# One decoder stack kernel: the late part of the last layer's shared expert, its sums, its loads and its last stores rearranged

## The reference, cut to what matters

```python
logits = x @ router_w.T                      # 8 experts, 2 chosen for each token
combine = ...                                # weight of each expert for each token, 0 if not chosen
out_e = silu(x @ gate_w[e]) * (x @ up_w[e]) @ down_w[e]          # 352 hidden columns
moe_out = sum over e of combine[:, e] * out_e
shared = silu(x @ s_gate_w + s_gate_b) * (x @ s_up_w + s_up_b) @ s_down_w + s_down_b   # 704 hidden columns
x = x + tanh(g_ffn[1]) * (moe_out + shared)  # x on the right inside is layernorm(x)
```

## Time and profile before

| | us |
|---|---|
| median of 3 runs | 1297.12 (1293.11 to 1299.21) |
| the profiled execution | 1299.26 |
| its span | 1297.6 |
| late part: first gate matmul to the end of the span | 1224.70 to 1297.6 |
| granted TensorE clock, mean over the span | 0.94 |

### The profile page before, as it was taken

How to read it: one execution, slowest core, us unless ns; L and a number is a source line. 1 busy time by engine, 2 the same in 40 slices (tenths; PEclk the granted TensorE clock), 3 DMA queues, 4 the chain that set the end, 5 groups by cost and what they waited for, 6 DMA issues and landing times. The chain is left out here.

```text
span 1297.6 us, 19278 instructions
## 1 busy us (share of the span) xinstructions
PE 1101.2 (85%) x6093; PEld 524.5 (40%) x6111; DVE 758.0 (58%) x1420; ACT 665.2 (51%) x1010; POOL 459.9 (35%) x503
## 2 busy tenths in 40 slices
PE   0567688897689999999999658699979999999894
PEld 0334444453324234334323124354446655556441
DVE  6888876764786675575565356644434454452245
ACT  6888887795235665565575625231314434434320
POOL 1101433322300422323323410616328888870071
PEclk9987899998779999999999878889989999999998
DMA  9125800000102112011010022104644444442484
GB/s 322 67 97 146 316 1 2 1 1 9 59 24 58 40 31 75 27 30 45 25 35 21 18 76 67 45 2 155 258 135 156 146 147 148 150 145 81 142 287 153
DMA packets 70653, 121.37 MB, mean 94 GB/s; under 512 B 16996, under 2 KB 30692, under 8 KB 70072
## 3 DMA queue, kind: packets, MB, share of 16 engines
q1 hardware_dynamic: 61032, 88.38, 20.9%
q0 software_dynamic: 9264, 31.92, 7.5%
q10 hardware_dynamic: 288, 0.20, 0.1%
HBM read 73.81 MB, written 38.65 MB: 87 GB/s over the span
## 5 line engine op out<-in xcount | busy, mean ns | idle before, releaser
L1240 ACT ACTIVATE prob<-p_col,mask_col,any_key 128x512 f32<-128x512 f32 x256 | 185.8, 778 | 110.4 <-PE p_col L1371 108.9
L1438 DVE CUSTOM_DVE_ANT_0 ajunk<-p_row,mask_row 128x512 bf16<-128x512 f32 x256 | 166.9, 685 | 72.3 <-PE p_row L1321 71.9
L1334 PE MATMUL p_out<-prob,v 128*64 128x512 f32 x512 | 139.0, 621 | 0.1
L1321 PE MATMUL p_row<-ks,early_place 99*128 99x512 f16 x256 | 100.4, 395 | 13.3 <-DVE top L1438 12.1
L1160 POOL TENSOR_TENSOR o<-sum_a,rec 32x512 f32<-32x512 f32 x30 | 37.9, 1264 | 195.1 <-DMA rec<-inv_d 193.0
L1371 PE MATMUL p_col<-early_place,ks 101*128 101x512 f16 x256 | 96.1, 388 | 0.8 <-ACT prob L1240 0.3
L2373 DVE SCALAR_TENSOR_TENSOR shid<-s_up,ssilu 128x352 f32<-128x352 f32 x39 | 20.5, 525 | 118.3 <-PE s_up L2286 118.3
L2308 PE MATMUL s_down<-mw,shT 128*128 (+1 forms) x351 | 82.2, 379 | 1.1 <-ACT shT L2231 1.1
L2286 PE MATMUL s_gate<-mw,sxT 128*128 x468 | 78.3, 318 | 4.2 <-ACT sxT L2237 3.3
L2375 DVE TENSOR_TENSOR shidr<-shid,shidr 128x352 f16<-128x352 f32 x39 | 66.9, 1715 | 21.5 <-ACT shidr L2221 21.5
L2286 PE MATMUL s_up<-mw,sxT 128*128 x468 | 77.4, 316 | 0.0
(11 more groups left out here) (318 smaller groups left out, 2220.3 us busy)
## 6 DMA issues: line engine op xcount, KB each, us to landing
x_slots<-nought SPq DMA_DIRECT2D x3, 3328.0 KB, 20.8
xin<-x_slots SPq DMA_DIRECT2D x39, 256.0 KB, 2.7
y_slots<-y SPq DMA_DIRECT2D x39, 256.0 KB, 2.1
early_place<-in_ctx SPq DMA_DIRECT2D x8, 1024.0 KB, 5.7
mstg<-in_L_ffn_gate_w POOLq DMA_DIRECT2D x7, 704.0 KB, 4.9
mstg<-in_L_ffn_up_w POOLq DMA_DIRECT2D x7, 704.0 KB, 5.1
x<-in_x SPq DMA_DIRECT2D x4, 1024.0 KB, 7.4
w<-in_L_ffn_w SPq DMA_DIRECT2D x1, 4096.0 KB, 18.4
```

The source lines that it names most:

```text
L1240: nc.scalar.activation(prob[s % 4][:, c, :], p_col[c][:], ACT.Exp, bias=mask_col[:, b, k:k + 1], scale=any_key[:, b:b + 1]).then_inc(t_exp, 1)
L1321: nc.tensor.matmul(p_row[g % 2][:], qs[0:ROWS_R, j, g, t * P:(t + 1) * P], ks[b % 2][0:ROWS_R, g, :], start=True, stop=True).then_inc(t_ro ...
L1334: mm = nc.tensor.matmul(p_out[pr][c * 2 * DH:(c + 1) * 2 * DH, :], v1[b % 2][:, k, g, :], prob[n % 4][:, c, :], start=(k == 0), stop=(k == ...
L1438: nc.vector.tensor_tensor_reduce(junk[:, g % 2, :], p_row[g % 2][:], mask_row[:, blk // HPG, :], 1.0, -3e38, ALU.add, ALU.max, top[blk % 2 ...
```

## The change

- SP: `first_up`, a new buffer, gets the first 128 up columns of unit 0 at the stage's start in two DMAs of 128 KB, whose rows in memory are 256 bytes long. The wait for the last down product is gone. The store of the last `y` is issued ahead of the up weights of unit 0. The last batch's result goes out in two stores of 512 KB.
- PE: the first up group reads `first_up`. Down sums both units of a token tile in one bank: 18 matmuls for tile 0, then tile 1, 2 and 3. The four sums have a bank each, the two of `p_down` and the two of `p_gate`. Ahead of the first of them PE waits for all six hidden groups and for both units' down weights.
- DVE: four adds in place of eight, two behind `combine(1)` and two behind `combine(2)`. The last `combine` is done in two halves of two token tiles.

```diff
+    first_up = sb(st, "first_up", [P, 2, KB, P], F16)
...
+    late_sum = [*p_down, *p_gate]
...
             sp.dma_start(first_gate[:], shared_d[0, :, :, G0:U0]).then_inc(e_pre, 16)
+            for h in range(2):
+                sp.dma_start(first_up[:, h, :, :], shared_d[0, :, h, U0:D0].rearrange("p (k i) -> p k i", i=EI)[:, :, 0:P]).then_inc(e_pre, 16)
...
             body(PAIRS_OF_TILES, 0)
-            sp.wait_ge(e_down, TILES)
+            store(PAIRS_OF_TILES, 0)
             sp.dma_start(late_w[0][:, :, U0:D0], shared_d[0, :, :, U0:D0]).then_inc(e_lu, 16)
-            store(PAIRS_OF_TILES, 0)
             sp.dma_start(late_w[1][:, :, G0:D0], shared_d[1, :, :, G0:D0]).then_inc(e_lv, 16)
...
-            for b in range(B):
+            for b in range(LATE_B):
                 sp.wait_ge(e_sum, b + 1)
                 sp.dma_start(out_d[b], x[:, b * TPB:(b + 1) * TPB, :]).then_inc(e_out, 16)
-            sp.wait_ge(e_out, 16 * B)
+            for half in range(2):
+                t0 = half * TPB // 2
+                sp.wait_ge(e_sum, LATE_B + half + 1)
+                sp.dma_start(out_d[LATE_B][:, t0:t0 + TPB // 2, :],
+                             x[:, LATE_B * TPB + t0:LATE_B * TPB + t0 + TPB // 2, :]).then_inc(e_out, 16)
+            sp.wait_ge(e_out, 16 * (B + 1))
...
+                        here = n == 0 and (at == G0 or m == 0)
+                        if here:
+                            pe.wait_ge(e_pre, 16 * 5)
+                        else:
+                            pe.wait_ge(*((e_lu, 16) if n == 0 else (e_lv, 16)))
...
-            late_down(0, e_ld0)
-            late_down(1, e_ld1)
+            pe.wait_ge(e_ld0, 32)
+            pe.wait_ge(e_ld1, 32)
+            pe.wait_ge(e_hl, TILES + 2 * EB)
+            pe.wait_ge(e_y, TILES)
+            for t in range(TPB):
+                for n in range(2):
                     for m in range(EB):
                         for hs, hm in passes:
-                            mm = nc.tensor.matmul(p_down[t % 2][:], late_hT[n][hs][0:rows(m), m, t * P:(t + 1) * P],
+                            mm = nc.tensor.matmul(late_sum[t][:], late_hT[n][hs][0:rows(m), m, t * P:(t + 1) * P],
...
+                                                  start=(n + m + hs + hm == 0), stop=(n == 1 and m == EB - 1 and hs == 1))
+                mm.then_inc(e_down, 1)
...
+            def combine(b, t0=0, t1=TPB):
...
             combine(1)
             late_add(0)
+            late_add(1)
             combine(2)
-            late_add(1)
-            dve.wait_ge(e_y, TILES + 2 * TPB)
-            combine(LATE_B)
+            late_add(2)
+            late_add(3)
+            dve.wait_ge(e_y, TILES + TPB)
+            combine(LATE_B, 0, TPB // 2)
+            combine(LATE_B, TPB // 2, TPB)
```

More of the change, by code:

```diff
@@ L2334, in late_gate_up @@
                     c = EB * n + m
[L2335 to L2338, removed]
+                    for at, bank, done, free in ((G0, p_gate, e_gate, e_silu), (U0, p_up, e_up, e_hid)):
+                        here = n == 0 and (at == G0 or m == 0)
[3 more added lines that the diff above has]
+                            pe.wait_ge(*((e_lu, 16) if n == 0 else (e_lv, 16)))
                         pe.wait_ge(free, TILES + max(c - 1, 0))
-                        src = first_gate if n == 0 and at == G0 else late_w[n]
                         for k in range(KB):
@@ L2343, in late_gate_up @@
                                 q = at + k * EI + m * P
-                                mm = nc.tensor.matmul(bank[c % 2][0:rows(m), :], src[:, hs, q:q + rows(m)], late_T[hm][:, k, :],
+                                if n == 0 and at == G0:
+                                    lhs = first_gate[:, hs, q:q + rows(m)]
+                                elif here:
+                                    lhs = first_up[:, hs, k, :]
+                                else:
+                                    lhs = late_w[n][:, hs, q:q + rows(m)]
+                                mm = nc.tensor.matmul(bank[c % 2][0:rows(m), :], lhs, late_T[hm][:, k, :],
                                                       start=(k == 0 and hs + hm == 0), stop=(k == KB - 1 and hs == 1))
                         mm.then_inc(done, 1)
[L2348 to L2352, removed]
+            late_gate_up(0)
+            late_gate_up(1)
+            pe.wait_ge(e_ld0, 32)
[4 more added lines that the diff above has]
+                for n in range(2):
                     for m in range(EB):
                         for hs, hm in passes:
-                            mm = nc.tensor.matmul(p_down[t % 2][:], late_hT[n][hs][0:rows(m), m, t * P:(t + 1) * P],
+                            mm = nc.tensor.matmul(late_sum[t][:], late_hT[n][hs][0:rows(m), m, t * P:(t + 1) * P],
                                                   late_w[n][0:rows(m), hm, D0 + m * D:D0 + (m + 1) * D],
[L2357 to L2361, removed]
-            late_down(0, e_ld0)
-            late_down(1, e_ld1)
+                                                  start=(n + m + hs + hm == 0), stop=(n == 1 and m == EB - 1 and hs == 1))
+                mm.then_inc(e_down, 1)
         @block.vector
@@ L2406, in late_low, with late_add @@
                                                late_hT[n][0][0:rows(m), m, :], ALU.mult, ALU.subtract).then_inc(e_hl, 1)
[L2408 to L2414, removed]
+            def late_add(t):
+                dve.wait_ge(e_down, TILES + t + 1)
+                xt = x[:, TPB * LATE_B + t, :]
+                nc.vector.scalar_tensor_tensor(xt, late_sum[t][:], gate_dn[:], xt, ALU.mult, ALU.add).then_inc(e_y, 1)
+            def combine(b, t0=0, t1=TPB):
                 dve.wait_ge(e_gathered[b], 16 * 2 * TPB)
                 for s in range(2):
-                    for t in range(b * TPB, (b + 1) * TPB):
+                    for t in range(b * TPB + t0, b * TPB + t1):
                         ins = nc.vector.scalar_tensor_tensor(x[:, t, :], gathered[:, t, s, :], share[:, s, t:t + 1], x[:, t, :], ALU.mult, ALU.add)
```

## The result

| | before | changed |
|---|---|---|
| median of 7 runs, us | 1296.60 | 1285.18 (1282.40 to 1288.16) |
| ratio, 95% interval | | 0.9912 (0.9891 to 0.9933) |
| profiled execution, us; its span | 1299.26; 1297.6 | 1285.99; 1284.3 |
| late part: first late gate matmul to the end | 72.90 | 60.73 |

Forecast were 1284.5 and a range of 1279.5 to 1290.5. The difference, 0.9%, is small but clear of the noise: the interval of the ratio leaves 1 outside. The late part takes 12.17 us less. The remaining 1.13 of the profiles' difference lies before it: the last stage already starts at 954.92 and not 956.15, in code that the change does not touch.

What follows compares the result with a forecast made beforehand. Late part bound by a wait for up weights, then PE alone, then DVE and PE in turns. Gains 4.64 + 8.2 + 1.3 = 14.1 us gave 1283.0 from the median; 1.4 for the clock made 1284.5, range 1279.5 to 1290.5.

Steps and rivals of the forecast that it cites:

- the charge for the clock: Ahead of down: a new PE idle time of 2.2 us may lower the clock; half of 2.8 us charged.
- The hole ahead of the first up group: Late part, PE: waiting for up weights loses 2.79 us, the lowered clock 1.85; early loading gains 4.64 us.
- The slack for the fourth block: Late part, up 1: its weights, issued behind the moved store, land at 1231.3, 1.2 us ahead of need.
- Down, one bank for each token tile: Late down products: 72 matmuls run through without waiting for DVE, 16.6 us in place of 24.81, gain 8.2 us.
- The gathers: POOL, late part: start about 2.8 us earlier; the last lands at 1273.8, 0.8 us before `combine(3)`.
- the 1283.0 of the held clock: Whole kernel: time in us forecast from the median before if the clock stays at full speed throughout down.
- the moved store covers 2.0 us: Last `y` store: without issuing it earlier, the last gather would land at 1276.6, after `combine(3)` should start at 1274.6.
- The halves: End of the kernel: last batch combined and stored in two halves, gain 1.3 us, bounds 0.5 and 2.1.
- The new loads: Stage's start: two early loads of small pieces delay POOL's expert weights by 1 us, costing the end nothing.
- the first, the falling clock: Start of down: clock falls in most runs, 1285 to 1286 us; 75% together with the forecast.
- The second, a gather or the weights at the end of a wait: Late part: a late gather gives 1285.0 or 1286.5 us, late up weights 1286.5 to 1288; chance 15%.
- The others: Parts not adding up, 1290.6 to 1297 us, 6%; slower through tile loop stalls, 2%; PE stalling between down tiles, 2%.

Runs made afterwards that it cites:

- e1: Changed kernel without the early load of the first up weights, which come behind the last store; ratio to the kernel before 0.9924, late part 89.16 us.
- a0: The changed kernel run again without edits on another chip; median 1333.96 us, ratio to the kernel before 0.9924.
- e3: Changed kernel with ten added matmuls, results unused, filling PE's idle time ahead of down; ratio to the kernel before 0.9896.
- e7: Kernel before with only the down sums in one bank per token tile and the changed kernel's adds; ratio to the kernel before 0.9941.
- e10: Changed kernel with two tiles' unit 0 done early, last gathers counted in halves, last y stored behind the up weights; median 1317.67 us, ratio to before 0.9796.
- e2: Changed kernel with the last y stored behind the up weights again; median 1328.3 us, ratio to the kernel before 0.9883.
- e2b: Changed kernel with the last y stored behind the up weights, a second time on another chip; ratio to the kernel before 0.9895.
- e9: Changed kernel with its 32 gathers replaced by plain copies, routed part of the result left out; late part 60.70 us, ratio to the kernel before 0.9716.
- e4: Changed kernel with PE doing unit 0 of two token tiles while the last hidden group is made; ratio to the kernel before 0.9891.
- b0: The kernel before, profiled again on one of the experiments' chips; late part 97.75 us.

## Why the prediction was right

The mechanism was right in its three parts, and each part has its own piece of the late part. The sizes need more care. The gain of the late part was 12.2, forecast 12.7 with the charge for the clock; the medians differ by 11.4, forecast 12.6. That 1284.5 and 1285.2 lie so near is in part luck: the clock was charged with a middle value that neither of its outcomes gives.

**The hole ahead of the first up group**: forecast 4.64, measured 4.47, and e1 brings it back at +3.7 with the clock held. The slack for the fourth block held too: the up weights were issued at 1224.87 and landed 4.7 later, 1.8 ahead of the block and not 1.2, and no wait for them is in the trace.

**Down, one bank for each token tile**: at full clock the forecast was 24.8 less 16.6. The profiles with the clock held show 16.9 (a0, e3, e7), so the term was over by 0.2 to 0.3; most of it is that PE starts 0.25 behind the last low part and not 0.05. The mechanism, PE running through while DVE waits for tile 3, is in the rows above: DVE waits 0.95 ahead of add 3, forecast 0.9.

**The clock.** I could not choose between hold and fall and charged 1.4, half of 2.8. It fell in the changed kernel's profile and cost 1.7 to 1.8, the lower of the two prices named. In the five profiles with all of down ahead of PE it fell three times, at idle times shorter than those at which it held; in e10 it fell after 2.83, in e7 it held after 2.67. That agrees with the rule of the Trainium skill, "TensorE: Matmul & The Clock Gate", that the monitor runs free of the kernel: the length of the idle time alone does not decide.

**The gathers.** They started 2.96 earlier against the first late gate (forecast 2.8). But from the first to the last took 42.7 and not 40.1, as one issue took 3.16 us. It began at 1246.15, 0.39 behind the start of `combine(0)` on DVE. The same is in e2, e2b and e10: an issue that began 0.14 to 0.28 behind the start of `combine(0)` took 3.27 to 3.41 us, and in no other profile does one take over 2. So the 0.8 of slack that I had given them was 0.24. This is the forecast's weakest step. Had the clock held, PE would have been done 1.7 earlier, but `combine(3)` would have waited for the gather that landed at 1275.3: by these rows the 1283.0 of the held clock was out of reach, and the fall cost the end 0.24 and not 1.7. The step "the moved store covers 2.0 us" is argued only. That the gathers were not on the path of the changed kernel its own rows show, where `combine(3)` follows add 3 at once. e9 without gathers agrees: it starts `combine(3)` at 51.86 behind the first late gate against 51.97.

**The halves**: 1.39 against 1.3; the landing of 512 KB took the 2.8 that the line gave.

**The new loads**: POOL's first split began 9.46 behind the stage's start and not 8.13, so 1.3 later (taken: 1), and the tile loop to the first late gate took 268.65 against 268.55. Cover as said.

**The signs.** One was written down wrongly: the first gather "3.4 after the last `y` is ready" is, by the forecast's own sum, 3.4 behind the first late gate (6.2 less 2.8). There it came at 3.3; behind the last `y` it came at 2.4.

**The rivals**: the first, the falling clock, came in the profile, and stands within the forecast. The second, a gather or the weights at the end of a wait, missed by 0.24. The others did not come on the first chip. None of mine named what lengthens the first piece by 26 us on the other chips. The forecast of 1284.5 would have been out by 49 there, while the ratio, 0.991 to 0.992, held.

## What to carry to other kernels

Two sums that go through the same banks in turn make the producer wait for the consumer's whole queue. Here a bank for each sum brought 6.3 of 12.2 us (7.3 in e7, where the clock held), more than the load that was moved (4.5). The new idle time that such a join makes ahead of a long block can be filled with work that is ready (e4: 3.1 us in its piece). But first find what comes next behind the engine that you speed up: in the changed kernel it was a gather, 0.24 us behind PE.

Cut a stage at two or three instructions that every version has. The middle pieces agreed to 0.1 us between kernels on different chips (16.90, 16.89, 16.91), where the executions of one kernel spread by up to 12 us (a0).

## What the runs showed of the hardware that was not expected

On the three chips of the experiments, in every profile with indirect DMAs in the late part, engines other than POOL stand idle without a wait while POOL issues them; in the two profiles of the first result they don't. In a0 PE takes 0.7, 1.4, 2.1 or 2.8 us for a matmul and its weights, and ACT and DVE lose up to 32.6 and 17.6 us in one wait. It hits the late part (+25 us in b0 and a0) and the scatter as well: from the first indirect DMA of the scatter to the start of the last stage b0 and a0 take 94.7 and 95.9 us, before and changed on the first chip 73.7. With plain copies of the same bytes, at a higher rate, it is gone from the late part.

Which engine is hit differs between the orders (PE in a0, DVE and ACT more in e2 and e2b); what decides it is not shown. Whether instructions came late is not shown either: the one 16 KB block that the instruction queue loads in the first piece comes 16.6 us behind the first late gate in a0, 16.2 in the changed kernel on the first chip and 15.8 in e9. The cause inside the chip was not found.
